# Moving a 5x5 depthwise convolution from TensorE to VectorE and GpSimd, with a new place for the key sums and another form of the LayerNorm factor

## What is computed

```
# layer 1, on the image x[n]: window attention with a local convolution
q, kv = projections of 16 x 16 windows of 2 x 2 pixels
r_idx = top_k(mean_q @ mean_k.T, 4)             # each window picks four windows
attn  = softmax(q . k[r_idx]);  out = attn . v[r_idx]   # 8 heads of 16 channels
lepe  = depthwise 5x5 convolution of v, one filter per channel
x     = x + out + lepe + b_lepe
h1 = relu(depthwise 3x3(fc1(x)));  x = x + fc2(h1)
# layer 2, on 1024 tokens of 128 channels: 4 heads, scores times a distance band
t = t + (softmax(scores * band) @ v) @ Wo       # of (t - mean) / sqrt(var + eps)
# layer 3: 8 experts, two per token
t = u + sum over e of combine[:, e] * expert_e(u)   # u = t plus its LayerNorm
```

## Time and profile before

| what | value |
|---|---|
| timed runs, median (lowest to highest) | 1887.87 us (1883.82 to 1893.44) |
| span of the profiled execution | 1907.9 us |
| TensorE matmuls, busy | 1678.3 us, 88% |
| GpSimd, busy | 1143.4 us, 60% |
| VectorE, busy | 1083.3 us, 57% |
| ScalarE, busy | 926.9 us, 49% |
| mean granted clock of TensorE | 0.919 of full speed |
| GpSimd's idle time ahead of its gathers | 375.0 us, of which 357.9 until the window table is stored |

### The profile page before, as it was taken

One profiled execution on the slowest core, in us unless ns is written; L12 is line 12 of the kernel. 1 busy time (PEld: TensorE's weight loads), 2 busy tenths in 40 slices (PEclk: granted clock), 3 DMA queues, 4 the chain that ended last, 5 costly groups with the idle time before them and its releaser, 6 DMA issues.

```text
span 1907.9 us, 48873 instructions
## 1 busy us (share of the span) xinstructions
PE 1678.3 (88%) x19584; PEld 1100.7 (58%) x19584; DVE 1083.3 (57%) x2437; ACT 926.9 (49%) x1289; POOL 1143.4 (60%) x653
## 2 busy tenths in 40 slices
PE   2906989899899989899899999999898999998997
PEld 1502557665566647666576656666576656664565
DVE  3483657554765657554765647555665657531754
ACT  0001259423873249523783249632693339623872
POOL 2583999169961899259970899339990799500000
PEclk9557889899998999899998999899998989998998
DMA  3303000040002100030001300030000300000000
GB/s 119 123 11 102 34 12 2 1 146 9 6 2 89 59 12 2 1 123 25 12 2 40 108 12 2 2 123 26 12 2 24 111 12 2 2 12 2 1 2 12
DMA packets 32343, 66.73 MB, mean 35 GB/s; under 512 B 6240, under 2 KB 19552, under 8 KB 31968
## 3 DMA queue, kind: packets, MB, share of 16 engines
q1 hardware_dynamic: 22880, 29.80, 5.0%
q0 software_dynamic: 9216, 33.56, 4.9%
HBM read 46.56 MB, written 12.58 MB: 31 GB/s over the span
## 4 chain that ended last, share of the span: by engine, by line
PE 64%; DVE 12%; ACT 8%; issue 7%; POOL 5%; another core or an unknown queue 2%; SPq 1%; DVEq 1%; DMA 0%; ACTq 0%; POOLq 0%
PE psB L437 11%; PE psB L602 9%; PE psA L504 9%; PE psB L567 8%; PE psA L651 6%; PE psB L620 5%; DVE STACKED L1183 3%; ACT PT L819 3%; ACT P L811 3%; PE psB L576 3%; PE psB L586 3%; PE psA L452 2%; DVE PT L1254 2%; POOL KV L1322 2%
## 5 line engine op out<-in xcount | busy, mean ns | idle before, releaser
L1134 DVE CUSTOM_DVE_ANT_0 P<-psB,W 128x1024 f32<-128x1024 f32 x256 | 313.6, 1225 | 145.9 <-PE psB L437 121.4
L1322 POOL TENSOR_TENSOR KV<-KVSEL,Q 128x1024 f32<-128x1024 f32 x120 | 284.6, 2404 | 36.1 <-DVE S L1004 21.0
L811 ACT ACTIVATE P<-P,NEGMAX 128x1024 f32<-128x1024 f32 x256 | 293.5, 1147 | 18.7 <-DVE NEGMAX L1142 17.4
L602 PE MATMUL psB<-W,P 128*128 128x128 f32 x2048 | 279.0, 278 | 21.8 <-ACT P L811 21.8
L1309 POOL DMA_INDIRECT KVSEL<-window_table,CHOSEN x64 | 60.5, 945 | 375.0 <-DMA window_table<-KV 357.9
L1357 POOL TENSOR_TENSOR PROD<-PROD 128x1024 f32<-128x1024 f32 x180 | 274.4, 1524 | 14.1
L602 PEld LDWEIGHTS psB<-W,P 128*128 128x128 f32 x2048 | 223.0, 140 | 87.2 <-issue 56.5
L819 ACT ACTIVATE PT<-psB 128x1024 f32<-128x1024 f32 x256 | 261.3, 1021 | 12.4 <-PE psB L602 9.2
L437 PE MATMUL psB<-TN,W 128*128 128x512 f32 (+1 forms) x512 | 248.3, 619 | 14.4 <-DVEq L1186 11.8
L1254 DVE SCALAR_TENSOR_TENSOR PT<-psB,PT 128x128 f32<-128x128 f32 x512 | 138.2, 344 | 116.6 <-PE psB L620 82.4
L437 PE MATMUL psB<-STACKED 96*128 96x512 f32 x512 | 186.3, 445 | 17.9 <-DVEq L1187 17.7
(11 more groups left out here) (129 smaller groups left out, 2348.3 us busy)
## 6 DMA issues: line engine op xcount, KB each, us to landing
window_table<-KV SPq DMA_DIRECT2D x8, 1024.0 KB, 7.4
X<-x_by_window_dram SPq DMA_DIRECT2D x8, 512.0 KB
XLEPE<-x_dram SPq DMA_DIRECT2D x8, 512.0 KB, 4.3
XLEPE<-P SPq DMA_DIRECT2D x128, 32.0 KB, 1.9
out_dram<-PT SPq DMA_DIRECT2D x8, 512.0 KB, 4.1
W<-packed_dram SPq DMA_DIRECT2D x1, 3714.5 KB, 11.6
KVSEL<-window_table,CHOSEN POOLq DMA_INDIRECT x64
FC<-packed_dram SPq DMA_DIRECT2D x8, 64.0 KB, 2.2
```

The costliest lines, as they stand in the source:

```text
L602: mm = pe.transpose(ps[:, t * 128:(t + 1) * 128], P[:, i % P_BUFFERS, t * 128:(t + 1) * 128], ident)
L811: act.activation(P[:, b, :], P[:, b, :], ACT.Exp, bias=NEGMAX[:, b, 1:2], accum_out=L[:, q, h:h + 1]).then_inc(p_ready, 1)
L1134: dve.tensor_tensor_reduce(P[:, b, :], ps[:], w("band", at, at + TOK), 1.0, -3.0e38, ALU.mult, ALU.max, NEGMAX[:, b, 0:1]).then_inc(free, 1)
L1322: pool.tensor_tensor(PRODUCTS[i % 2].rearrange("p (k c) -> p k c", c=C), KVSEL[:, t, keys, 0:C], Q[:, t, q, :].unsqueeze(1).broadcast_to([ ...
```

## The change

All images but the first leave TensorE's convolution out. VectorE does 17 taps of image m as one fused instruction each, straight into XLEPE (`vector_taps`): five behind experts 2 to 6 of the stage before, six among the first six key sums, six behind the scores 5, 9, 13, 17, 21 and 25. GpSimd does the other eight (`pool_taps`) at the head of its stage, ahead of the gathers, into a tile of their own, POOL_LEPE, which is the upper half of PROD; a step behind score 28 on VectorE (`merge`) adds it to XLEPE. All key sums move behind the experts, to the head of the stage. V's two matmuls and V_PAD move forward, from the middle of the experts to the second LayerNorm. The variance becomes one matmul of 512 columns, and the factor exp(-ln(var + eps) / 2) on ScalarE over all of them, so that neither the reciprocal nor the spreading matmul is left; logarithm and exponential share a table.

```
@@ GpSimd @@
+        POOL_LEPE = PROD[:, TOK:2 * TOK]
+            def pool_taps(m):
+                pool.wait_ge(v_ready, PX * (m + 1))
+                pool.wait_ge(pv_done, 1)
+                if not isinstance(m, int):
+                    pool.wait_ge(lepe_merged, m - 1)
+                acc = POOL_LEPE.rearrange("c (y x) -> c y x", y=SIDE)
...
             def values(m, t):
                 done = VALUE_STEPS * pooled_before(m, t)
                 pool.wait_ge(e_ready, WTILES * m + t + 1)
+                if t == 0 and not (isinstance(m, int) and m == 0):
+                    pool.wait_ge(lepe_merged, m)
...
             def window_stage(m):
+                pool_taps(m)
                 for t in range(WTILES):
                     gathers(m, t)
...
-                last_taps(m)
@@ VectorE @@
+POOL_TAPS = 8
+VECTOR_TAPS = TAPS5 - POOL_TAPS
+TAPS_BEHIND_EXPERTS = (2, 3, 4, 5, 6)
+TAPS_AMONG_KEYS = 6
+TAPS_BEHIND_SCORES = (5, 9, 13, 17, 21, 25)
+MERGE_BEHIND_SCORES = 28
-EARLY_STEPS = 8
-LATE_STEPS = 2
+LATE_STEPS = 4
...
+                    dve.scalar_tensor_tensor(out=image, in0=V_PAD[:, dy:dy + SIDE, dx:dx + SIDE], scalar=col("lepe_w", tap),
+                                             in1=image, op0=ALU.mult, op1=ALU.add).then_inc(vector_tap, 1)
+                def merge():
+                    dve.wait_ge(vector_tap, VECTOR_TAPS * m)
+                    dve.wait_ge(lepe_done, (POOL_TAPS - 1) * m)
+                    dve.tensor_tensor(XLEPE[:], XLEPE[:], POOL_LEPE, ALU.add).then_inc(lepe_merged, 1)
...
-                    steps = second_half(second)[EARLY_STEPS:]
-                later = second_half(first)[:EARLY_STEPS] if first is not None else []
+                    steps = second_half(second)
+                taps = vector_taps(second)[len(TAPS_BEHIND_EXPERTS):] if second is not None else []
+                first_taps = vector_taps(first)[:len(TAPS_BEHIND_EXPERTS)] if first is not None else []
...
-                run(steps, len(steps) - LATE_STEPS)
+                for i in range(len(steps) - LATE_STEPS):
+                    run(steps, 1)
+                    run(taps, int(i < TAPS_AMONG_KEYS))
...
+                    if u in TAPS_BEHIND_SCORES or u == MERGE_BEHIND_SCORES:
+                        run(taps, 1)
...
-                    run(later, {5: 1, 6: 1, 7: EARLY_STEPS - 2}.get(e, 0))
+                    run(first_taps, int(e in TAPS_BEHIND_EXPERTS))
@@ TensorE @@
-                        lepe_taps(second, groups[:count])
...
+                    mm = pe.matmul(ps[:, 0:HALF], w("mean_w").broadcast_to([128, C]), SQ[:, half * HALF:(half + 1) * HALF], **whole)
...
+                        if name == ("centred", 1, 1):
+                            a_windows(first)
+                            for h in range(2):
+                                a_values(first, h)
+                        if name == "router":
+                            a_logits(first)
...
-                        if name == ("hidden", 3):
-                            for h in range(2):
-                                a_values(first, h)
@@ ScalarE @@
+                act.activation(SQ[:, cols], psB[s][:, 0:HALF], ACT.Ln, bias=col("eps")).then_inc(b_free[s], 1)
+                act.wait_ge(b_free[s], turn + 1)
+                act.activation(SQ[:, cols], SQ[:, cols], ACT.Exp, scale=-0.5).then_inc(rstd_ready, 1)
...
-                    if first is not None and e == 3:
-                        a_values(first)
```

More of the change, by code:

```diff
@@ L102, in __init__ @@
         self.place = {name: i % slots for i, name in enumerate(body)}
+        once = [name for name, _ in first if name not in self.place]
+        self.place.update({name: i % slots for i, name in enumerate(once)})
         self.first = first + [(name, ahead(name) - 1) for name in body if ahead(name) > 0]
@@ L380, in spread_lepe, with image_traffic @@
                                          LEPE_OUT[32 * c:32 * c + 32, at:at + 256]).then_inc(lepe_in, 16)
-            def image_traffic(n, second, first, after):
-                if second is not None:
-                    spread_lepe(second)
+            def image_traffic(n, first, after):
                 if first is not None:
@@ L516, in a_first_half @@
                         a_project(m, t, p)
-                for h in range(2):
-                    a_values(m, h)
             def emit(name, n):
@@ L1129, in scale_scores @@
                     b = u % P_BUFFERS
-                    if u == 2 and second is not None:
-                        dve.wait_ge(lepe_in, 16 * LEPE_DMAS * (second + 1))
                     at = TOK - 128 - 128 * (u // HEADS_C)
@@ L1165, in stages_b_to_d @@
                 dve.sem_inc(free, 1)
-                run(steps, 1)
-                for half in range(2):
-                    spread(0, half)
+                run(steps, 2)
                 for half in range(2):
                     normalise(0, half)
-                run(steps, 1)
+                run(steps, 2)
                 ps, free = arrived("v")
@@ L1198, in stages_b_to_d @@
                 normaliser(TT - 1)
-                assert not steps
+                assert not steps and not taps
                 run(front, 1)
@@ L1289, in _ @@
             to_stream(0)
[L1290 removed]
+            for step in first_half(1) + vector_taps(1)[:len(TAPS_BEHIND_EXPERTS)]:
                 step()
```

137 lines of the change are left out of this document (56 added, 81 removed).

## The result

The changed kernel takes 2348.65 us (median of four runs, 2343.27 to 2350.85), the kernel before 1885.84 us (four runs, 1871.5 to 1893.44): a ratio of 1.247, with a 95% interval from 1.242 to 1.252. The forecast was 2335 us, in a range from 2265 to 2405. The profiled execution spans 2349.0 us, 441.1 more than that of before.

What follows compares the result with a forecast made beforehand. The prediction took a repeating chain of waits, 218.4 us an image, with GpSimd's value products as key, to bound the kernel. Terms: 452 - 49 + 4 + 39 + 3, less 2, is 447; 1907.9 + 447 - 20 = 2335 us, range 2265 to 2405.

Steps and rivals of the forecast that it cites:

- The wait that is added: GpSimd's value products wait for VectorE's merge behind score 28: 65.5 us an image, 59 in the seventh, 452 in all.
- What is taken away: Gains from both LayerNorms, the front and V's matmuls leaving the expert stage: 33 + 5 + 11 = 49 us.
- The front: Last expert's matmuls to fc2's end: without taps TensorE waits for ScalarE, a gain of 1 us x 5.
- What is added beside the wait: VectorE's 17 taps and GpSimd working beside VectorE: 4 us at the scores, 39 in the router, 3 in image 1.
- The router: About eight two-operand VectorE instructions slowed by GpSimd's taps: 6.5 us for each of six images, 39 us.
- The lumps of taps among the scores: Six VectorE taps and the merge, 9 us in 22.4 us of idle time: 0.5 us lost an image, 4 in all.
- Rival (1): TensorE bounds the kernel and GpSimd's wait is harmless: 1850 us; chance 0.05 together with (2).
- fc2 hides it, with about 6 us to spare: Taps among the key sums cost nothing except in image 1, since fc2 covers the delay with about 6 us spare.
- The sum: All terms together add 447 us to the profiled 1907.9; 20 taken off for the timed median gives 2335 us.
- (2): GpSimd's wait is already satisfied by an earlier image's merge, so nothing waits: 1850 us; chance 0.05 together with Rival (1).
- (3): VectorE and GpSimd exclude each other strictly, in the router and among the key sums: 81 us more, 2416; chance 0.10.
- (4): The exclusion costs the router nothing: 2293 us; counted as the lower half of the forecast's 0.84.

Runs made afterwards that it cites:

- experiment 1: Changed kernel with the merge of GpSimd's taps moved from behind score 28 to behind the first key sum: 1985.77 us, ratio to the kernel before 1.056.
- ln_psum: ln_only with the factor's exponential written back to PSUM instead of SBUF: 1843.02 us, ratio to the kernel before 0.979.
- experiment 3: Changed kernel with GpSimd's second to eighth tap cut to one of 32 image rows: 2290.95 us, ratio 1.217.
- experiment 4: experiment 1 with seven VectorE taps moved behind scores 22 to 30: 1953.18 us; the same with GpSimd's taps cut as in experiment 3: 1894.76 us.
- ln_only: Kernel before with only the new LayerNorm factor (one variance matmul, logarithm, exponential): 1853.0 us, ratio 0.983; in a second run 1844.42 us, 0.981.
- early_late_thin: experiment 1 with seven VectorE taps moved behind scores 22 to 30 and GpSimd's second to eighth tap cut to one image row: 1894.76 us, ratio 1.008.
- shared_keys: ln_only with the taps shared as GpSimd nine, VectorE three (behind experts 3, 4 and 7), TensorE thirteen: 1844.73 us, ratio 0.981.

## Why the prediction was right, step by step

**The wait that is added.** Right in place and size: 65.5 us an image were forecast, 65.0 measured, and 57 for the seventh against 59 (the router at 289.9 us behind the sums, 232.8 before). The products take 73.5 us beside an idle VectorE (74.2 assumed). GpSimd's wait is 88 us, where some 100 were named as a sign. One sentence of the step is wrong: that the merge "has to" stand behind score 28, since it needed the 17 VectorE taps. An addition does not care for its order, and experiment 1 shows that it can stand 126 us earlier in the period (82 us behind the sums and not 208). With that sentence I missed that the price was a line's place and not the change's.

**What is taken away.** The first LayerNorm and the scores' start gain 6.4 us where I put 5.5, and I gave all of it to the taps that leave TensorE and none to the new factor. From fc2's end to the product with V's weights the runs have all four cases: 15.6 us with the taps and the old factor, 9.2 with the old factor alone (the last image), 10.6 with the taps and the new factor (ln_psum, 1065.0 to 1075.6), 8.0 with the new factor alone (the changed kernel). So either part alone brings most of the gain, and they do not add up; that the factor counts for nothing is the term that was wrong, and the size came out in part by luck. It also needs GpSimd to stand idle, as it does there: where GpSimd is busy (experiment 1) the two normalisations take 1.22 and 2.45 us and not 0.69 each, and the gain of 6.4 is one of 3.6 (24.4 us against 27.96). The second LayerNorm, cancelled to zero, gained 2.1 us.

The expert stage became 2.8 us shorter, where V's matmuls had been put at 1.88. This hangs on one tap: the fourth of those behind the experts meets GpSimd's first key products. In the changed kernel it takes 2.43 us, in experiment 1 5.58, beside two key products in a row:

```profile
1320.76 2.43 DVE L1069 SCALAR_TENSOR_TENSOR XLEPE<-V_PAD,W,XLEPE 128x1024 f32<-128x1024 f32 x1 [0.23 <-DVE PT L1250]
```
```profile
1103.92 5.58 DVE L1073 SCALAR_TENSOR_TENSOR XLEPE<-V_PAD,W,XLEPE 128x1024 f32<-128x1024 f32 x1 [0.23 <-DVE PT L1255]
```
```profile
1103.68 4.73 POOL L1323 TENSOR_TENSOR KV<-KVSEL,Q 128x1024 f32<-128x1024 f32 x2
```

There the stage takes 33.4 us, and nothing is gained. **The front** had the wrong sign: a gain of 1 us was forecast, and the stretch from the last expert to fc2's end lost 0.6 + 2.9 us. TensorE, without taps to fill its gaps, is busy for 27.02 of 33.67 us ahead of fc2 (32.85 of 33.03 before), and fc2 then runs at a granted clock of 0.71 in 10.06 us instead of 7.14 at 1.00 (8.6 to 10.1 in the five full periods). I had weighed that only for the second LayerNorm, although have fc2 at 8.83 us in the last image.

**What is added beside the wait.** The router: 6.5 us forecast, 6.1 measured and taken away again by experiment 3. The projections lost another 1.3, for which I had nothing. The lumps of taps among the scores: 0.5 us forecast, 0.0 measured, but only because GpSimd stood in its wait; beside the value products the stretch grew from 74.6 to 81.1 us (experiment 1). Rival (1) said 1883 us at worst if only the wait went away, and 1986 were measured; by experiment 4 the taps among the scores are 33 us of this miss of 103. "fc2 hides it, with about 6 us to spare" (the taps among the key sums) was too kind. Here are ScalarE, which takes the first tile's exponential ahead of the last 3x3 results, and TensorE's last 3x3 pass in the changed kernel:

```profile
1359.65 0.63 ACT L744 ACTIVATE S<-S 128x512 f32<-128x512 f32 x1 [11.98 <-DVE S L996]
```
```profile
1348.05 11.24 PE L568 MATMUL psB<-H_PAD,DIAG 32*32 32x512 f32 x288 [2.76 <-ACTq L754]
```

The exponential starts 0.36 us after the 3x3 pass has ended (1359.29): nothing was spare, and fc2 starts at most 1 us late for it. The maximum's subtraction ahead of it (L996) took 2.88 us beside GpSimd, 0.98 in the same place before.

**The sum.** 447 us on the span were forecast and 441.1 measured: the errors cancel (an image: front +4.6, projections +1.3, second LayerNorm -2.1, first -0.9, experts -0.9, the wait, router and scores about -0.5 each). The five full periods make 319.8 us of it, for which the terms give 320.6. Outside them the errors are larger: the start of the program is 9.1 us shorter, for which the forecast had no term (ln_only has the same, 8.7), and image 1's period grows by 76.9 us, more than the others, since its gathers also wait for its taps. The step that did not hold is the 20 us taken off for the profiled execution of before: the changed kernel's trace, 2349.0, lies at its median. Why the trace of before lies 20 us off stays open. The timed runs of the kernel before that have a clock on record go from 1868.6 us at 0.935 to 1892.7 at 0.921; the trace, at 0.919, has 1907.9, more than this trend gives.

**The rivals.** (2) is refuted by the wait itself. (3) took the exclusion as strict; single instructions do wait out a whole GpSimd instruction, but the router's eight lose 0.8 us each on average, since some fall into a gap or find the engine's product near its end. (4) is refuted by experiment 3. (1) put the gain from the freed TensorE at up to 138 us; the runs with the wait and most collisions gone (early_late_thin) and with fewer taps on TensorE (shared_keys) show no gain from it. The Trainium skill (Perfetto Trace Analysis, section Identifying the Most-Contended Engine) says to optimise the engine with the highest occupancy first; with TensorE taken by its matmul busy time, which the same section calls no good measure of how close it is to its limit, these runs do not bear that out.

## What to carry to other kernels

When a scratch tile is squeezed into another's space, the wait for its release belongs to the price, and it is set by where the reader of the scratch stands in its engine's order: put that reader as early as its own inputs allow. Work moved off the busiest engine is a gain only if that engine's stage is the one that ends last, and the work costs more at its new place wherever a neighbouring engine excludes it; time the parts of a mixed change apart, since here one of them (the LayerNorm factor, 1.8% faster) was hidden under 24.7% of loss. A gap that is filled with other matmuls may be worth its cost: with taps beside the 3x3 pass fc2 ran at a granted clock of 1.00 in 7.14 us, without them, in the changed kernel, at 0.71 to 0.83 in 8.6 to 10.1.

## What the runs showed of the hardware that was not expected

- A VectorE instruction with both operands in SBUF that meets a running GpSimd product waited for that product's whole rest: 4.06 us for 0.69 (512 columns), 3.83 for 1.28 (a tap), 1.42 for 0.17 (8 columns). A tap that met two products in a row waited for both, 5.58 us. With one operand in PSUM all 32 of the same form took 686 to 689 ns. The Trainium skill (SBUF — State Buffer, section Who interferes with whom) says that a VectorE instruction with at most one SBUF input, outside its 2-port modes, does not contend with GpSimd; these runs agree.
- The same program runs loop periods of 208 or of 215 us (ln_only). In the long ones one such wait of VectorE (4.05 to 4.07 us for 0.69) goes before an idle TensorE (3.83 us), and the granted clock from fc2 to the first scores is 0.88 and not 1.00; with the factor in PSUM it is 1.00 in all five full periods.
